# Attention scores from two float32r parts on two halves of the partitions, in place of three bfloat16 parts

## The chip, the cores and the metric

The kernel runs on one core of a Trainium2 chip. The metric is device microseconds of one launch; less is better. The page and the trace call the engines PE (TensorE's matmuls), PEld (its weight loads), DVE (VectorE), ACT (ScalarE), POOL (GpSimd) and SP (SyncE, which here only issues DMAs).

## What is computed

A transformer of two layers on `x` of 4 sequences (batches) x 1024 tokens x 128 features, all in float32. Cut to what matters:

```
x = x + attn0(layernorm(x))      # 16 heads of 8 features, causal mask, softmax, then Wo
x = x + experts(layernorm(x))    # router softmax, top 2 of 8 experts, 352 hidden
x = x + attn1(layernorm(x))      # 16 query heads, 4 key/value heads, no mask; q, k times a rotary-like factor
x = x + ffn(layernorm(x))        # 512 hidden, a sine term, relu
scores = q @ k^T;  weights = softmax(scores / sqrt(128));  out = weights @ v      # per head, 1024 x 1024
```

## The kernel before

The engines run programs of their own and meet only at semaphores. The stages follow one another: projection of layer 0 (`project(0)`), attention 0, experts, projection of layer 1, attention 1, feed-forward.

**The split.** TensorE multiplies bfloat16 faster than float32, so `project` writes each of q and k as a sum of three bfloat16 parts (SPL = 3): ACT rounds the first part (line 873), DVE subtracts it (line 1126), ACT rounds the second (line 882), DVE takes the rest (line 1130). POOL writes the parts to DRAM (`write_parts`, lines 451 and 453). SP loads them back (`load`, lines 344 and 348) so that the 8 features of a head stand in 72 partitions: the 3 x 3 products of parts, 8 rows each, are summed by one matmul with a contraction of 72 rows. That is `Q[0:CROSS, slot, j, :]` and `K[0:CROSS, slot, j, :]`, CROSS = 72, for head j of a quad.

**The work of attention.** A quad is four heads (j = 0 to 3) of one batch; there are 4 batches x 4 quads = 16 quads in each layer, g = 4b + q. Per quad there are two passes over the scores:

- `pass_a` (lines 560 to 576): for each head and each block i of 128 queries, the scores of 128 queries x all keys go to two PSUM banks, and DVE takes the maximum of each row (`row_max`, line 1152). 32 such units per quad; head j changes only after 8 units. In layer 0 only keys up to the diagonal are computed, and a matmul of the bfloat16 identity with a triangle of -1e30 (line 574) adds the mask.
- `pass_b` (lines 593 to 609): the transposed scores, 128 keys x up to 512 queries, of the heads j = 0, 1, 2, 3 in turn. Three more rows (72 to 74) hold minus the row maximum in three parts, and ones on the other side, so that the matmul subtracts it. ACT takes the exponential (line 921). In layer 0 the diagonal block gets its mask from line 607.
- `pv` (lines 611 to 624): the weights times V, in float32, four heads side by side in four groups of 32 array columns (line 620).

The row maximum gets there by `negmax_split` on DVE (lines 1155 to 1166), `negmax_turn` on PE (line 629), a copy on ACT (line 905) and one DMA from SP (`negmax_rows`, line 355).

**The order.** PE, DVE and ACT all follow one list of letters per layer (`ORDERS`, lines 147 to 151): `b` one head of pass B, `a` one unit of pass A of the next quad, `p` one `pv`, and letters for the turns. PE runs it in this order:

```
if ev[0] == "B":
    pass_b(g, q, ev[1], ev[2])
elif ev[0] == "A":
    ...
elif ev[0] == "PV":
    pv(g, q, ev[1])
```

Before the first quad, 40 units of pass A run alone (lines 643 to 652). The batches are a hardware loop on each engine (`Fori`, line 694 on PE), the last one written out.

Of the kernel before, what the change touches and what calls it, by code (L numbers as in the profile page):

```python
# [18 lines left out]
F32 = mybir.dt.float32  # L19
BF16 = mybir.dt.bfloat16  # L20
# [4 lines left out]
P = 128  # L25
# [16 lines left out]
SPL = 3  # L42
CROSS = SPL * SPL * HD
KROWS = CROSS + SPL
SLOTS = 4
PR = 8
HALF = 512
# [7 lines left out]

TWO_ONES = float(np.uint32(0x3F803F80).view(np.float32))
# [102 lines left out]
QUAD_LOADS = 2 * SPL * SPL + 1  # L159


def build(nc, h_in, Wqvk, Wo0, router_w, gate_proj, up_proj, down_proj, w_q, w_k, w_v, w_o, g_rms,
          W1, b1, phases, w_real, w_imag, W2, b2, rope, out):
    q_parts = [nc.dram_tensor(f"q_parts{l}", (SPL, P, B * S), BF16, kind="Internal").ap() for l in range(2)]
    k_parts = [nc.dram_tensor(f"k_parts{l}", (SPL, r, B * S), BF16, kind="Internal").ap()
               for l, r in enumerate((P, KV * HD))]
    x_dram = h_in.rearrange("b (t p) d -> p (b t) d", p=P)
    out_dram = out.rearrange("b (t p) d -> p (b t) d", p=P)

    with ExitStack() as ctx:  # L170
# [3 lines left out]
        def sem(name):  # L174
            return ctx.enter_context(nc.semaphore(name))
# [5 lines left out]
        Q = sb("Q", [P, SLOTS, 4, S], BF16)  # L181
        K = sb("K", [P, SLOTS, 4, S], BF16)
# [4 lines left out]
        negmax = sb("negmax", [P, SPL, 32], BF16)  # L187
        negrest = sb("negrest", [P, 32])
        negmaxT = sb("negmaxT", [SPL * 32, P], BF16)
        rden = sb("rden", [P, 4, 4])  # L190

        spare = Q[:, :, :, :].rearrange("p s j n -> p (s j n)").bitcast(F32)
# [5 lines left out]
        spare_k = K[:, :, :, :].rearrange("p s j n -> p (s j n)").bitcast(F32)  # L198
# [3 lines left out]
        identb = sb("identb", [P, P], BF16)  # L202
        causal = sb("causal", [P, P], BF16)
# [39 lines left out]
        rest = probs[:, 2:4, :]  # L243
        parts = spare[:, B * S:B * S + 2 * SPL * GW].bitcast(BF16)\
            .rearrange("p (two a c n) -> p two a c n", two=2, a=2, c=SPL)
# [20 lines left out]

        def score_a(n):
            return ps[:, 2 * n:2 * n + 2, :].rearrange("p b n -> p (b n)")

        def turn_bank(unit):  # L270
# [8 lines left out]
        consts, k_ones = sem("consts"), sem("k_ones")  # L279
# [3 lines left out]
                 "qk_sb", "v_taken", "hi_done", "rest_done", "mid_done", "split_done", "scores", "max_done",  # L283
                 "negmax_ready", "negmaxT_psum", "negmaxT_ready", "negmax_rows", "scoresT", "exp_done", "pv_done",
                 "o_copied", "o_turned", "attn_done")
        from_one = ("rstd_ready", "qk_sb", "v_taken", "rest_done", "split_done", "o_copied", "o_turned",
# [29 lines left out]
        def ones_rows(a, b):  # L316

            return K[64:96, a:b, :, :].rearrange("p s j n -> p (s j n)").bitcast(F32)
# [7 lines left out]
        def _(sp):  # L326
# [6 lines left out]
            for l in range(2):  # L333
                sl = s[l]

                def load(b, q):

                    for a in range(SPL):

                        heads = q_parts[l][a, :, bass.ts(b, S)].rearrange("(h i) n -> i h n", i=HD)  # L340
                        heads = heads[:, 4 * q:4 * q + 4, :] if l == 0 else heads[:, q:H:KV, :]
                        for r in range(SPL):
                            row = (a * SPL + r) * HD
                            sp.dma_start(Q[row:row + HD, q, :, :], heads).then_inc(loaded[l][q], 16)

                            keys = k_parts[l][r, :, bass.ts(b, S)].rearrange("(h i) n -> i h n", i=HD)
                            keys = keys[:, 4 * q:4 * q + 4, :] if l == 0 else keys[:, q:q + 1, :]
                            sp.dma_start(K[row:row + HD, q, 0:keys.shape[1], :], keys).then_inc(loaded[l][q], 16)
                    w = (HD + 1) * (4 if l == 0 else 1)
                    sp.dma_start(V[:, q, :, 0:w], v1[:, bass.ts(b, 8), w * q:w * q + w]).then_inc(loaded[l][q], 16)  # L350

                def negmax_rows(q, g):

                    sp.wait_ge(sl["negmaxT_ready"], g + 1)
                    sp.dma_start(Q[CROSS:KROWS, q, :, :].rearrange("c j (i n) -> c (j i) n", n=P),
                                 negmaxT[:, :]).then_inc(sl["negmax_rows"], 16)


                sp.wait_ge(k_ones, 2)
# [3 lines left out]
                for q in range(2):  # L363
                    load(0, q)
# [4 lines left out]
                load(0, 2)  # L369
                negmax_rows(0, 0)  # L370

                def batch(b, final):
                    for q in range(4):
                        g = 4 * b + q
                        if q == 0 or not final:
                            sp.wait_ge(sl["o_turned"], 2 * g + AT_ONE)
                            load(b if q == 0 else b + 1, (q + 3) % 4)
# [3 lines left out]
                with sp.Fori(0, B - 1) as b:  # L381
                    batch(b, False)
# [9 lines left out]
        def _(pool):  # L392
            own = Chain(pool, pool_own, own_wait=True)
            own.done(pool.memset(ident[:, :], 0.0))
            own.done(pool.memset(identb[:, :], 0.0))
            own.done(pool.memset(causal[:, :], 0.0))
# [3 lines left out]
            for m in (ident, identb):  # L400
                pool.affine_select(out=m[:, :], in_=m[:, :], compare_op=ALU.not_equal, fill=1.0, base=0,
                                   pattern=[[-1, P]], channel_multiplier=1).then_inc(consts, 1)
            pool.affine_select(out=causal[:, :], in_=causal[:, :], compare_op=ALU.is_ge, fill=MASKED, base=0,
                               pattern=[[-1, P]], channel_multiplier=1).then_inc(consts, 1)
# [4 lines left out]
            pool.wait_ge(consts, 5)  # L409
# [46 lines left out]
            own.done(pool.memset(ones_rows(0, 2), TWO_ONES))  # L456
# [50 lines left out]
        def _(pe):  # L507
# [6 lines left out]
            def project(l):  # L514
# [7 lines left out]
                read = sl["rest_done"] if l == 0 else sl["qk_sb"]  # L522
# [32 lines left out]
            def attention(l):  # L555
# [4 lines left out]
                def pass_a(quad, slot, j, i):  # L560
# [3 lines left out]
                    kj = j if l == 0 else 0  # L564
# [861 lines left out]
```

## Time and profile before

| what | value |
|---|---|
| median of 3 runs | 2203.51 us (2200.15 to 2205.18) |
| profiled execution, span from first to last instruction | 2193.3 us |
| profiled execution, its own time (end of the last instruction on the trace's own clock) | 2203.8 us |
| PE matmul busy | 2032.1 us, 93% |
| DVE busy | 1464.8 us, 67% |
| ACT busy | 1189.7 us, 54% |
| mean granted PE clock | 0.951 of full speed |
| stages, roughly | projection 0: to 82 us; attention 0: 82 to 650; experts: 650 to 1190; projection 1: 1190 to 1241; attention 1: 1241 to 2070; feed-forward: to the end |

The 10.5 us between span and own time lie around the first and last instruction. Busy times are unions of an engine's instructions. Ends of matmuls are modelled, so the distance between the starts of neighbouring matmuls tells the rate better than their duration does.

### The profile page before, as it was taken

To read this page: it belongs to the slowest core of one execution; us is meant where nothing else is said; L and a number is where in the kernel's file an instruction comes from. 1 tells how busy PE (TensorE), PEld (TensorE's weight loads), DVE (VectorE), ACT (ScalarE), POOL (GpSimd) and SP (SyncE) were. 2 spreads that over 40 slices of the span, in tenths; PEclk is the share of its full clock that TensorE was granted. 3 is DMA by queue.
4 is the path that set the end of the run, shared out by engine and by line. 5 is a ranking of instruction groups with operands and counts; after the bars stand their busy time and mean duration, and the time that the engine had idled before them with its cause. 6 is when DMAs were issued, how large, how long until landed. Compare 5 with 4: busy or idle time off the path is not lost. (4 is left out here: it accounts for less than half of the span.)

```text
span 2193.3 us, 38142 instructions
## 1 busy us (share of the span) xinstructions
PE 2032.1 (93%) x11744; PEld 893.1 (41%) x11744; DVE 1464.8 (67%) x2435; ACT 1189.7 (54%) x2374; POOL 142.6 (7%) x216
## 2 busy tenths in 40 slices
PE   4599899999999999999999789999999999999876
PEld 2244344344435666666665212222222222222355
DVE  5677577577744545455554988887886887886186
ACT  2256466466672222222322337776776777777776
POOL 3100000000000000000000100000000000000065
PEclk9689899799999999999998869999998999999998
DMA  7533324143100000000000411011111111100000
GB/s 205 129 43 38 48 27 51 28 50 41 12 2 1 0 0 0 0 0 0 0 0 1 115 15 16 16 16 17 18 26 17 16 15 16 16 2 1 1 15 24
DMA packets 75282, 56.82 MB, mean 26 GB/s; under 512 B 43120, under 2 KB 57328, under 8 KB 75120
## 3 DMA queue, kind: packets, MB, share of 16 engines
q1 hardware_dynamic: 64416, 38.62, 12.0%
q0 software_dynamic: 3072, 10.23, 1.4%
q10 hardware_dynamic: 7632, 5.88, 1.0%
q8 instruction: 93, 1.52, 0.3%
q14 instruction: 69, 0.57, 0.1%
HBM read 38.65 MB, written 12.32 MB: 23 GB/s over the span
## 5 line engine op out<-in xcount | busy, mean ns | idle before, releaser
L1152 DVE TENSOR_REDUCE rowmax<-ps 128x1 f32<-128x1024 f32 (+7 forms) x1024 | 971.3, 987 | 288.3 <-PE ps L571 140.0
L921 ACT ACTIVATE probs<-ps 128x512 f32<-128x512 f32 (+3 forms) x1792 | 860.2, 558 | 367.8 <-PE ps L604 217.1
L604 PE MATMUL ps<-Q,K 75*128 75x512 bf16 (+3 forms) x1792 | 547.5, 366 | 32.6 <-ACT probs L921 16.8
L571 PE MATMUL ps<-K,Q 72*128 72x512 bf16 (+3 forms) x1792 | 545.6, 380 | 34.7 <-DVE rowmax L1152 31.0
L620 PE MATMUL ps<-probs,V 128*9 128x512 f32 (+3 forms) x3584 | 450.2, 561 | 0.0
L604 PEld LDWEIGHTS ps<-Q,K 75*128 75x128 bf16 x1792 | 167.3, 99 | 398.7 <-ACT probs L921 281.3
L957 ACT ACTIVATE Q<-ps 128x512 f32<-128x512 f32 (+1 forms) x192 | 114.4, 596 | 324.5 <-PE ps L730 314.0
L571 PEld LDWEIGHTS ps<-K,Q 72*128 72x128 bf16 x1792 | 152.5, 100 | 326.4 <-DVE rowmax L1152 188.9
L1266 DVE TENSOR_TENSOR Q<-ps,Q 128x512 f32<-128x512 f32 (+1 forms) x192 | 130.2, 688 | 136.6 <-PE ps L733 136.4
L733 PE MATMUL ps<-Q,wu 128*128 (+3 forms) x384 | 197.2, 595 | 1.6 <-DVE Q L1266 1.6
L730 PE MATMUL ps<-Q,wg 128*128 (+3 forms) x384 | 196.9, 594 | 1.0 <-DVE attn L1177 1.0
L742 PEld LDWEIGHTS ps<-wd,Q 128*128 128x128 f32 (+1 forms) x1536 | 180.3, 191 | 28.3 <-issue 25.1
L742 PE MATMUL ps<-wd,Q 128*128 128x128 f32 (+1 forms) x1536 | 180.5, 274 | 0.0
L1278 DVE SCALAR_TENSOR_TENSOR x<-ps,ew,x 128x128 f32 (+1 forms) x256 | 72.2, 344 | 117.6 <-PE ps L742 117.6
L620 PEld LDWEIGHTS ps<-probs,V 128*9 128x9 f32 x3584 | 61.0, 89 | 149.2 <-ACT probs L921 85.6
L574 PE MATMUL ps<-causal,identb 128*128 128x128 bf16 x512 | 116.9, 231 | 0.0
L733 PEld LDWEIGHTS ps<-Q,wu 128*128 128x128 f32 (+1 forms) x384 | 68.0, 181 | 101.4 <-issue 83.1
L416 POOL TENSOR_SCALAR rtmp<-mv 128x4 f32<-128x4 f32 x16 | 3.4, 213 | 1601.8 <-DVE mv L1073 1601.8
L607 PE MATMUL ps<-identb,causal 128*128 128x128 bf16 x512 | 106.8, 225 | 0.0
L730 PEld LDWEIGHTS ps<-Q,wg 128*128 128x128 f32 (+1 forms) x384 | 65.2, 181 | 68.2 <-issue 68.2
L511 PE MATMUL ps<-ident,tokens 128*128 128x128 f32 x192 | 32.8, 298 | 42.5 <-DVE tokens L1106 30.1
L574 PEld LDWEIGHTS ps<-causal,identb 128*128 128x128 bf16 x512 | 52.4, 102 | 40.2 <-issue 8.4
(157 smaller groups left out, 1132.0 us busy)
## 6 DMA issues: line engine op xcount, KB each, us to landing
Q<-q_parts SPq DMA_DIRECT2D x288, 64.0 KB
K<-k_parts SPq DMA_DIRECT2D x144, 64.0 KB
q_parts<-Q POOLq DMA_DIRECT2D x16, 384.0 KB, 3.4
k_parts<-Q POOLq DMA_DIRECT2D x8, 384.0 KB, 7.6
V<-v SPq DMA_DIRECT2D x16, 144.0 KB
K<-k_parts SPq DMA_DIRECT2D x144, 16.0 KB
x<-in_L_attn_h_dram SPq DMA_DIRECT2D x4, 512.0 KB, 9.7
out_dram<-y SPq DMA_DIRECT2D x8, 256.0 KB, 2.3
```

The source lines that it names most:

```text
L571: last = pe.matmul(buf[:, c:e], Q[0:CROSS, slot, j, i * P:(i + 1) * P], K[0:CROSS, slot, kj, c:e], start=True, stop=not diag)
L574: last = pe.matmul(buf[:, w - P:w], identb[:, :], causal[:, :], start=False, stop=True)
L604: last = pe.matmul(ps[:, bank, c:HALF], K[0:KROWS, q, kj, t * P:(t + 1) * P], Q[0:KROWS, q, j, h * HALF + c:(h + 1) * HALF], start=True, s ...
L607: last = pe.matmul(ps[:, bank, c:c + P], causal[:, :], identb[:, :], start=False, stop=True)
L620: last = pe.matmul(ps[32 * j:32 * j + rows, PV_BANK, c:HALF], V[:, q, t, kj * rows:(kj + 1) * rows], probs[:, (4 * m + j) % PR, c:HALF], s ...
L730: pe.matmul(ps[0:w, par, :], wg[:, e, f:f + w], moving, start=True, stop=True).then_inc(moe["gate"], 1)
L733: pe.matmul(ps[0:w, 2 + par, :], wu[:, e, f:f + w], moving, start=True, stop=True).then_inc(moe["up"], 1)
L742: last = pe.matmul(ps[:, 4 + e % 2, k * D:(k + 1) * D], acts[0:w, e % 2, c, k * P:(k + 1) * P], wd[0:w, c, e, :], start=(c == 0), stop=(c ...
L921: act.activation(probs[:, (4 * m + j) % PR, c:HALF], ps[:, B_BANKS[(4 * m + j) % 3], c:HALF], ACT.Exp, scale=SCALE).then_inc(sl["exp_done" ...
L957: act.activation(gated[0:w, par, :], ps[0:w, par, :], ACT.Silu).then_inc(moe["silu"], 1)
L1152: dve.tensor_reduce(rowmax[:, par, 8 * j + i:8 * j + i + 1], score_a(i % 2)[:, 0:hd.keys(i)], AX, ALU.max).then_inc(sl["max_done"], 1)
L1266: dve.tensor_tensor(acts[0:w, e % 2, c, :], ps[0:w, 2 + par, :], gated[0:w, par, :], ALU.mult)\
```

## The change

SPL becomes 2 and the parts are float32 words. The first part is rounded by a write as float32r; the second is the float32 remainder. Q and K are float32r tiles. A head now needs 2 x 2 x 8 = 32 rows (ROWS), then one row (32) that is zero in Q and K, then two rows for minus the row maximum (KROWS = 35). Even heads stand at partitions 0 to 34, odd heads at 64 to 98 (LANE = 64), and Q and K have two heads' columns per slot in place of four. `pass_a` uses the 32 rows alone; `pass_b` all 35. The masks of layer 0 are two matmuls of 64 rows each in place of one of 128, on the half of the head. In the program, a matmul of pass A covers 32 rows x 128 columns of the array, one of pass B and of the masks 64 x 128, `pv` 128 x 32 as before, turns 128 x 128; before, all but `pv` were 128 x 128.

```diff
-SPL = 3
-CROSS = SPL * SPL * HD
+SPL = 2
+ROWS = SPL * SPL * HD
+CROSS = ROWS + 1
 KROWS = CROSS + SPL
+LANE = 64
...
-        Q = sb("Q", [P, SLOTS, 4, S], BF16)
-        K = sb("K", [P, SLOTS, 4, S], BF16)
+        Q = nc.alloc_sbuf_tensor_at("Q", [P, SLOTS, 2, S], F32R, offset=q_at)
+        K = nc.alloc_sbuf_tensor_at("K", [P, SLOTS, 2, S], F32R, offset=k_at)
...
+        def lane(j, rows):
+
+            return slice(LANE * (j % 2), LANE * (j % 2) + rows)
...
-                        last = pe.matmul(buf[:, c:e], Q[0:CROSS, slot, j, i * P:(i + 1) * P],
-                                         K[0:CROSS, slot, kj, c:e], start=True, stop=not diag)
+                        last = pe.matmul(buf[:, c:e], Q[lane(j, ROWS), slot, j // 2, i * P:(i + 1) * P],
+                                         K[lane(j, ROWS), slot, kj, c:e], start=True, stop=not diag)
                         if diag:
-                            last = pe.matmul(buf[:, w - P:w], identb[:, :], causal[:, :],
-                                             start=False, stop=True)
+                            for part in range(2):
+                                last = pe.matmul(buf[:, w - P:w], identb[lane(j, LANE), part, :],
+                                                 causal[lane(j, LANE), part, :], start=False, stop=part == 1)
...
-                    last = pe.matmul(ps[:, bank, c:HALF], K[0:KROWS, q, kj, t * P:(t + 1) * P],
-                                     Q[0:KROWS, q, j, h * HALF + c:(h + 1) * HALF], start=True, stop=not diag)
+                    last = pe.matmul(ps[:, bank, c:HALF], K[lane(j, KROWS), q, kj, t * P:(t + 1) * P],
+                                     Q[lane(j, KROWS), q, j // 2, h * HALF + c:(h + 1) * HALF],
+                                     start=True, stop=not diag)
                     if diag:
-                        last = pe.matmul(ps[:, bank, c:c + P], causal[:, :], identb[:, :],
-                                         start=False, stop=True)
+                        for part in range(2):
+                            last = pe.matmul(ps[:, bank, c:c + P], causal[lane(j, LANE), part, :],
+                                             identb[lane(j, LANE), part, :], start=False, stop=part == 1)
...
-                    for n in range(2):
-                        r = rows[n]
-                        act.wait_ge(sl["rest_done"], 2 * u + n + 1 + AT_ONE)
-                        act.activation(parts[0:r, half, n, 1, :], rest[0:r, n, :], ACT.Copy)\
-                            .then_inc(sl["mid_done"], 1)
```

Further parts, in words. `load` issues 8 DMAs for Q, 8 for K (each of 16 partition rows' worth of 4 KB instead of 32 of 2 KB) and 1 for V, 17 in place of 19; `negmax_rows` issues two DMAs, one per half. The first use of each slot also copies the zero row (2 DMAs), and 8 small DMAs at the start fill it in K from zeros in `probs`. DVE fills `probs` and K at the start over all partitions, POOL sets up the masks in 5 selects in place of 3. `negmax_split` has 2 operations in place of 4, and the row maxima are turned as a 128 x 128 float32 tile. SP's first batch is written out.

The PE program in a quad of layer 0 (one head of pass A, of pass B, and the start of a `pv`), before:

```order
L571 MATMUL ps<-K,Q 128x256 [waits max_done0]
L574 MATMUL ps<-causal,identb 128x128
L601 REGISTER_ALU
L604 MATMUL ps<-Q,K 128x384 [waits exp_done0]
L607 MATMUL ps<-identb,causal 128x128
L620 MATMUL ps<-probs,V 9x512 [waits exp_done0,o_copied0]
```

and now:

```order
L600 MATMUL ps<-K_50,Q_49 128x256 [waits max_done0]
L604 MATMUL ps<-causal,identb 128x128 x2
L631 REGISTER_ALU
L634 MATMUL ps<-Q_49,K_50 128x384 [waits exp_done0]
L639 MATMUL ps<-identb,causal 128x128 x2
L652 MATMUL ps<-probs,V 9x512 [waits exp_done0,o_copied0]
```

The order of the work is the same; each mask has become two matmuls.

The DVE program of one group of 512 tokens in the projection of layer 0, before (`probs` is the remainder, `Q` the parts):

```order
L1123 ISA
L1126 TENSOR_TENSOR probs<-ps,Q 128x512 [waits hi_done0,split_done0]
L1125 REGISTER_ALU
L1126 TENSOR_TENSOR probs<-ps,Q 128x512 [waits hi_done0]
L1130 TENSOR_TENSOR Q<-probs,Q 128x512 [waits mid_done0] x2
```

and now (`spare` is the parts):

```order
L1153 ISA
L1154 TENSOR_TENSOR spare<-ps,spare 128x512 [waits hi_done0]
L1153 REGISTER_ALU
L1154 TENSOR_TENSOR spare<-ps,spare 128x512 [waits hi_done0]
```

Two of four subtractions are gone, and the wait for ACT's second rounding with them.

## Rows read from the trace of the kernel before

**Rows 1.** The page, section 1: busy us (share of the span) xinstructions

```profile
PE 2032.1 (93%) x11744; PEld 893.1 (41%) x11744; DVE 1464.8 (67%) x2435; ACT 1189.7 (54%) x2374; POOL 142.6 (7%) x216
```

**Rows 2.** Busy by stretch (start:end, length, then each engine), attention 0, then 1

```profile
303.00:368.00 65.00, 64.32 (x533) 28.99 (x532) 48.86 (x81) 42.48 (x103) 0.00 (x0) 1.00 0.35 43
...
1531.00:1675.00 144.00, 142.34 (x799) 41.16 (x799) 118.80 (x121) 105.27 (x203) 0.00 (x0) 1.00 0.12 18
```

**Rows 3.** Timeline (start us, us), SP's DMA of the row maxima, one per quad

```profile
322.99 0.78 SPq L355 DMA_DIRECT2D Q<-negmaxT  x1
355.48 0.79 SPq L355 DMA_DIRECT2D Q<-negmaxT  x1
...
1579.42 0.78 SPq L355 DMA_DIRECT2D Q<-negmaxT  x1
1627.22 0.80 SPq L355 DMA_DIRECT2D Q<-negmaxT  x1
```

**Rows 4.** Timeline, PE in a quad of attention 1

```profile
1561.64 1.05 PE L620 MATMUL ps<-probs,V 128*9 128x512 f32 x8
1562.62 0.61 PE L571 MATMUL ps<-K,Q 72*128 72x512 bf16 x2
1563.07 0.60 PE L604 MATMUL ps<-Q,K 75*128 75x512 bf16 x2
1563.50 0.60 PE L636 MATMUL ps<-ident,oT 128*128 128x128 f32 x4
1563.94 0.38 PE L604 MATMUL ps<-Q,K 75*128 75x512 bf16 x1
1564.25 1.40 PE L620 MATMUL ps<-probs,V 128*9 128x512 f32 x8
```

**Rows 5.** Timeline, PE in the experts' stage, float32 matmuls (two records each)

```profile
900.83 0.72 PE L742 MATMUL ps<-wd,Q 128*128 128x128 f32 x5
901.38 1.02 PE L730 MATMUL ps<-Q,wg 128*128 x2
902.24 1.02 PE L733 MATMUL ps<-Q,wu 128*128 x2
```

**Rows 6.** Timeline, PE in a quad of attention 0

```profile
603.11 0.22 PE L607 MATMUL ps<-identb,causal 128*128 128x128 bf16 x1
603.17 0.22 PE L571 MATMUL ps<-K,Q 72*128 72x128 bf16 x1
603.23 0.22 PE L574 MATMUL ps<-causal,identb 128*128 128x128 bf16 x1
```

**Rows 7.** Timeline, pass A alone before attention 1: DVE, then PE

```profile
1254.89 9.42 DVE L1152 TENSOR_REDUCE rowmax<-ps 128x1 f32<-128x1024 f32 x8
```

```profile
1258.52 2.17 PE L571 MATMUL ps<-K,Q 72*128 72x512 bf16 x4 [0.19 <-DVE rowmax L1152]
```

**Rows 8.** Busy by stretch, pass A alone; the last three are clock, DMA share, GB/s

```profile
1242.00:1278.00 36.00, 31.57 (x62) 4.02 (x62) 36.00 (x31) 0.00 (x0) 0.83 (x2) 0.50 0.18 35
```

**Rows 9.** Groups by line, DVE in the projection of layer 1 (busy us, mean ns | idle)

```profile
L1130 DVE TENSOR_TENSOR Q<-probs,Q 128x512 bf16<-128x512 f32 (+1 forms) x16 | 10.3, 682 | 0.8
L1126 DVE TENSOR_TENSOR probs<-probs,Q 128x512 f32<-128x512 f32 (+1 forms) x16 | 10.2, 678 | 2.2 <-ACT Q L873 2.2
```

**Rows 10.** Timeline, ACT in the projection of layer 1

```profile
1233.36 1.15 ACT L873 ACTIVATE Q<-probs 128x512 bf16<-128x512 f32 x2 [1.26 <-DMA k_parts<-Q]
1234.81 1.22 ACT L882 ACTIVATE Q<-probs 128x512 bf16<-128x512 f32 x2 [0.15 <-DVE probs L1126]
```

**Rows 11.** Busy by stretch in the projection of layer 0 (DMA share, GB/s at the end)

```profile
50.00:55.00 5.00, 3.38 (x17) 2.12 (x16) 1.61 (x5) 1.24 (x3) 1.52 (x2) 1.00 0.81 212
```

**Rows 12.** Timeline, DVE at the start of a new batch of attention 0

```profile
262.68 0.62 DVE L1152 TENSOR_REDUCE rowmax<-ps 128x1 f32<-128x128 f32 x2 [12.41 <-issue]
```

**Rows 13.** Groups by line and form, PEld in the experts' stage

```profile
L730 PEld LDWEIGHTS ps<-Q,wg 128*128 128x128 f32 x4 | 0.7, 190 | 0.5 <-issue 0.5
```

More of the change, by code:

```diff
@@ L19 @@
 F32 = mybir.dt.float32
+F32R = mybir.dt.float32r
 BF16 = mybir.dt.bfloat16
@@ L168, in build @@
     out_dram = out.rearrange("b (t p) d -> p (b t) d", p=P)
+    q_at, k_at = (nc.bump_sbuf(SLOTS * 2 * S * 4)[0] for _ in range(2))
     with ExitStack() as ctx:
@@ L363, in _ @@
                 for q in range(2):
-                    load(0, q)
+                    load(0, q, first=True)
                 sp.wait_ge(sl["v_taken"], NG + AT_ONE)
@@ L368, in _, with batch @@
                     sp.wait_ge(sl["parts_written"][half], 32 * (NG // 2))
-                load(0, 2)
+                load(0, 2, first=True)
                 negmax_rows(0, 0)
-                def batch(b, final):
+                def batch(b, final, fresh=False):
                     for q in range(4):
@@ L376, in batch @@
                             sp.wait_ge(sl["o_turned"], 2 * g + AT_ONE)
-                            load(b if q == 0 else b + 1, (q + 3) % 4)
+                            load(b if q == 0 else b + 1, (q + 3) % 4, first=q == 0 and fresh)
                         if q < 3 or not final:
                             negmax_rows((q + 1) % 4, g + 1)
-                with sp.Fori(0, B - 1) as b:
-                    batch(b, False)
+                batch(0, False, fresh=True)
+                with sp.Fori(0, B - 2) as b:
+                    batch(b + 1, False)
                 batch(B - 1, True)
@@ L399, in _ @@
             own.done(pool.memset(power_b[:, :], -0.5))
[L400 to L404, printed above, removed]
+            own.done(pool.affine_select(out=ident[:, :], in_=ident[:, :], compare_op=ALU.not_equal, fill=1.0, base=0,
+                                        pattern=[[-1, P]], channel_multiplier=1))
+            for par in range(2):
+                rows = slice(LANE * par, LANE * par + LANE)
+                own.done(pool.affine_select(out=identb[rows, :, :], in_=identb[rows, :, :], compare_op=ALU.not_equal,
+                                            fill=1.0, base=0, pattern=[[LANE, 2], [-1, P]], channel_multiplier=1))
+                own.done(pool.affine_select(out=causal[rows, :, :], in_=causal[rows, :, :], compare_op=ALU.is_ge,
+                                            fill=MASKED, base=0, pattern=[[LANE, 2], [-1, P]], channel_multiplier=1))
             pool.affine_select(out=lower[:, :, :], in_=lower[:, :, :], compare_op=ALU.is_ge, fill=1.0, base=0,
@@ L872, in body @@
                             src = qk32[0:r, n, :]
[L873 removed]
+                        act.activation(parts[0:r, half, n, 0, :].bitcast(F32R), src, ACT.Copy)\
+                            .then_inc(sl["hi_done"], 1)
                     act.wait_ge(sl["v_out"], u + 1)
```

141 lines of the change are left out of this document (74 added, 67 removed).

## The prediction

> **What bounds the kernel now.** The page's busy line comes first: PE 93%, DVE 67%, ACT 54% [rows 1]. It mixes stages, so the second view is the busy time of stretches inside the two attentions, which hold some 1,400 of the 2,193 us: PE is busy 64.3 of 65 us and 142.3 of 144, DVE 48.9 and 118.8, ACT 42.5 and 105.3, all at the full clock of 2.4 GHz [rows 2]. PE sets the pace, and DVE comes next at 75% and 82%. The third view is the period of a quad, the distance between two DMAs of row maxima: 32.5 us in attention 0 and 47.8 us in attention 1 [rows 3].
>
> The fourth is what PE spends a quad on, read from distances between starts. A bfloat16 matmul of 512 columns takes 0.216 us (two of L604 in 0.43 us, start to start) [rows 4]; one of 128 columns 0.06 us, mask or score alike [rows 6]. A float32 matmul of 512 columns takes 0.86 us [rows 5], and a `pv` (eight records for four heads) 0.98 us from its start to the next matmul [rows 4]: the four heads run side by side, 0.86 us in all, and 0.12 us is left over. On the way in, the matmul before `pv` takes 0.31 us in place of 0.216 [rows 4]. So going between matmuls on 128 x 128 and on 128 x 32 of the array costs **about 0.10 us each way**. With this, attention 1 adds up: 128 score matmuls x 0.216 = 27.6, 16 `pv` x 0.86 = 13.8, 32 such switches = 3.2, turns (4 in 0.44 us [rows 4], twice) 0.9: 45.5 of the 47.8 us.
>
> **The change, part by part.**
>
> *Rate of a score matmul: nothing.* The trace has none in float32r. Bounds: 0.216 us for 512 columns as in bfloat16 [rows 4], or 0.86 us as in float32 [rows 5]; in between, a turn of float32 data takes 0.11 us for 128 columns [rows 4], twice bfloat16's. I take 0.216: the float32 matmul leaves two records, each with its own weight load [rows 5, 13], since both operands have to be cut in two there, and here the program has cut them beforehand. That the contraction falls from 72 to 32 rows is worth nothing: distance follows columns. A float32 weight load lasts 0.19 us [rows 13], but such loads keep up with matmuls 0.11 us apart (five in 0.55 us [rows 5]), so they hide behind 256 columns or more.
>
> *Two heads at once: a gain.* Neighbouring matmuls on different halves may run together, as the four heads of `pv` do. But order limits it. Pass A keeps its head for 8 units, so its two matmuls lie on one half. Pass B alternates, and walking the letters I count 22 free pairs of neighbouring `b` per quad in attention 1: 22 x 0.216 = 4.8 us. In attention 0 a mask must follow its score on the same half and holds up the next head; 4 pairs are left in the unmasked groups, -0.9 us, and 24 second masks that run beside the next head's score, -1.4 us.
>
> *Masks: a cost.* 64 per quad in attention 0 become 128: 64 x 0.06 = +3.8 us [rows 6].
>
> *Switches: the largest term.* Pass A now uses 32 rows of the array, pass B and the masks 64. Walking the letters around the quad, the size of the used array changes 84 times per quad in attention 0 (22 before) and 87 times in attention 1 (32 before): 62 and 55 more. The trace shows only the switch of columns. Bounds: 0, if a change of rows is free, and 0.19 us each, if the first float32 weight load cannot be brought forward [rows 13]. I take 0.10, from the nearest row [rows 4]: +6.2 and +5.5 us per quad.
>
> The Trainium skill, "TensorEngine Tiling", Key Properties, says that changing the tiling mode, and not just the tile, drains the engine, and lists 64 and 32 rows as different modes. The 0.10 us of `pv` agrees; for rows no run here shows it. By that rule the sum is the one below, and without it the first rival.
>
> *Sum of the quads.* Attention 0: 3.8 - 1.4 - 0.9 + 6.2 = +7.7; I take +7.0, since part falls where PE waits today. Attention 1: 5.5 - 4.8 = +0.7. Times 16: +112 and +11 us. DVE (32 x 1.18 = 37.7 us plus 1.5 of small work per quad of attention 1 [rows 7]) stays below 48.5.
>
> *Pass A alone.* 40 units ahead of each attention. In attention 1 DVE sets the pace, 1.18 us a unit; PE at 1.2 GHz needs 0.86 [rows 7] plus two switches: covered. In attention 0 a unit gets a mask (0.11 us at 1.2 GHz) and two switches, partly covered by DVE: +5 us.
>
> *Projections.* In layer 1 DVE loses 16 operations of 0.68 us [rows 9], and ACT a pair of 1.22 us per group [rows 10] on the loop between them; writes go from 384 to 512 KB for q. I take -12 of at most 10.9 + 8 x 1.2 = 20.5. In layer 0 the DMAs are the limit (0.81 busy, 212 GB/s [rows 11]), with a third more bytes in fewer, larger pieces: 0, within 8 either way.
>
> *With one answer.* `negmax_split` saves 0.4 us of DVE under PE. The second DMA of row maxima adds 0.8 us on SP [rows 3] behind a load of 17 DMAs in place of 19, microseconds before the next quad needs it. Should it be late, pass B would wait first. The early fills and POOL's selects precede data from DRAM. The stalls at a new batch, DVE without instructions for 12.4 us [rows 12], stay.
>
> Sum: 112 + 11 + 5 - 12 = **+116 us**. The profiled execution took 2203.8 us itself, span 2193.3, 0.3 above the median of 2203.5. So 2320 us.
>
> **Rivals.**
>
> 1. *Changing rows is free; faster.* Then attention 1 keeps -4.8 and its neighbouring `a` and `b` may overlap too, until waits for DVE (39.2 us per quad) hold it near 43.5 us: -4.2. In attention 0 the 3.8 us of masks against 2.3 of overlap, and some of A beside B: about 0. So -67 - 12 = 2125 us, up to 2200 if pairing disappoints. It decides below 0.04 us per switch. For it: only a switch of columns is shown, where the output side changes as well. Against: the same array has to be regrouped.
>
>    The Trainium skill, "TensorE: Matmul & The Clock Gate", Part 3, lets matmuls in different row groups start 4 ns apart; this supports the pairs in either case. The trace shows it only for columns.
>
> 2. *Float32r takes two passes or more; slower.* At twice the time per column attention 1 gains 13.8 us for A and some 7 for B per quad, attention 0 some 7.7 and 6: with the switches about 690 us, 2890 in all; at four passes over 3500. For it: the turns at 0.11 us. Against: one record per matmul in the new program.
>
> 3. *The clock falls; slower.* With 72 rows and matmuls on 0.86 of 1.18 us, pass A alone stayed at 1.2 GHz for its whole length [rows 7, 8]. If the sparser attention stayed there too, each quad would gain 30 us or more: over 3100. Against: quads with `pv` ran at 2.4 GHz, and at the lower clock the stream would get denser.
>
> 4. *The halves don't run together.* Then 4.8 and 2.3 us per quad come back: 2430 us.
>
> **Numbers.** My forecast 0.50, rival 1 0.28, rival 2 0.12, rival 3 0.05, rival 4 0.05. Both signs have weight: the likeliest case alone spans 2250 to 2400. The range leaves out rivals 2 and 3: from 2115 (rival 1 in full) to 2430 (rival 4, or switches at 0.16 us). About 0.2% is what a measurement of this kernel can tell from no change. Of rival 1, 0.26 is faster and 0.02 within 0.2%; of the forecast 0.02 each for faster and same: faster 0.28, same 0.04, slower 0.68.
>
> **What would show it.** Right: a quad near 39.5 us in attention 0 and 48.5 in attention 1; neighbouring `b` 0.01 us apart and then a gap; 0.3 us from an L634 matmul of 512 columns to an L600 one. Wrong: `a` and `b` on different halves starting together (rival 1); 0.43 us or more between two L600 matmuls of one unit (rival 2); clock 0.5 in the quads (rival 3); neighbouring `b` always 0.216 apart (rival 4).

## The result and the profile after

| | before | after |
|---|---|---|
| median | 2202.79 us (4 runs, 2200.15 to 2205.18) | 3527.82 us (4 runs, 3522.27 to 3532.10) |
| ratio to before | 1 | 1.601, 95% interval 1.596 to 1.606 |
| span of the profiled execution | 2193.3 us | 3527.0 us |
| mean granted PE clock | 0.951 | 0.613 |

The change makes the kernel 60% slower. The page of after, its busy line and its clock row (one digit for each fortieth of the span, tenths of full speed):

```profile
PE 3397.6 (96%) x12768; PEld 1446.6 (41%) x12768; DVE 1480.0 (42%) x2340; ACT 1218.6 (35%) x2342; POOL 143.7 (4%) x219
...
PEclk8555555555555589999985555555555555555589
```

PE is now 96% busy, and DVE and ACT do about the same work as in [rows 1] in a span 1.6 times as long. The clock row shows why: fives through both attentions, nines in the experts' stage between them and at the very end. Stretches of attention 0 and 1, and then all of attention 1 (start:end, length, PE, PEld, DVE, ACT, POOL busy, clock, DMA share, GB/s):

```profile
303.00:368.00 65.00, 65.00 (x305) 28.75 (x299) 21.84 (x35) 19.48 (x45) 0.00 (x0) 0.50 0.15 20
...
2459.00:2557.00 98.00, 97.66 (x267) 31.35 (x265) 40.57 (x38) 36.66 (x67) 0.00 (x0) 0.50 0.07 9
...
1889.00:3406.00 1517.00, 1497.86 (x4184) 480.95 (x4180) 603.89 (x591) 584.46 (x1070) 2.43 (x4) 0.51 0.05 7
```

Against [rows 2] PE does 305 matmuls in the same 65 us where it did 533, at 0.50 in place of 1.00, and the clock stays down for 1,500 us though PE has work the whole time. The period of a quad, from SP's DMAs of the row maxima (now two at a time):

```profile
549.28 1.31 SPq L372 DMA_DIRECT2D Q<-negmaxT  x2
620.88 1.29 SPq L372 DMA_DIRECT2D Q<-negmaxT  x2
...
2458.90 1.36 SPq L372 DMA_DIRECT2D Q<-negmaxT  x2
2556.96 1.29 SPq L372 DMA_DIRECT2D Q<-negmaxT  x2
```

71.6 and 98.1 us, where [rows 3] had 32.5 and 47.8 and the forecast 39.5 and 48.5. The whole difference lies here: from its first `pv` to its last, attention 1 takes 1517 us in place of 779 (+738), and attention 0 by the same measure 1128 in place of 543 (+585): 1323 of the 1334 us between the spans. Inside a quad of attention 1, PE (start, length, line, shape, how many):

```profile
2601.47 0.79 PE L634 MATMUL ps<-Q,K 35*128 35x512 f32 x1
2602.19 1.22 PE L600 MATMUL ps<-K,Q 32*128 32x512 f32 x2
2603.33 0.79 PE L634 MATMUL ps<-Q,K 35*128 35x512 f32 x2
2604.05 1.90 PE L652 MATMUL ps<-probs,V 128*9 128x512 f32 x8
```

At half clock 512 columns take 0.43 us, twice the 0.216 of [rows 4]. The two L634 of the third line, an even and an odd head, need 0.72 us from the start of the first to `pv`: one matmul of 0.43 and 0.29 more, which is taken up below with e1. So the two halves do run together, and float32r does go in one pass. The two L600 take 1.14 us to the next line, more than two times 0.43 and one switch.

### The profile page after: what moved, and what is told of

Same layout as the page of the kernel before. It is cut to its first block and busy times, and to the rows that moved or that the text cites. A ratio compares the mean times of both kernels' runs of the same rounds, so it can differ in the third digit from the quotient of the medians.

```text
span 3527.0 us, 39737 instructions
## 1 busy us (share of the span) xinstructions
PE 3397.6 (96%) x12768; PEld 1446.6 (41%) x12768; DVE 1480.0 (42%) x2340; ACT 1218.6 (35%) x2342; POOL 143.7 (4%) x219
## 5 line engine op out<-in xcount | busy, mean ns | idle before, releaser
L600 PE MATMUL ps<-K,Q 32*128 32x512 f32 (+3 forms) x1792 | 1036.2, 663 | 19.6 <-DVE rowmax L1176 17.7
L634 PE MATMUL ps<-Q,K 35*128 35x512 f32 (+3 forms) x1792 | 867.6, 715 | 24.5 <-ACT probs L948 14.5
L652 PE MATMUL ps<-probs,V 128*9 128x512 f32 (+3 forms) x3584 | 754.8, 938 | 0.0
L600 PEld LDWEIGHTS ps<-K,Q 32*128 32x128 f32 x1792 | 445.6, 297 | 591.0 <-issue 371.9
L634 PEld LDWEIGHTS ps<-Q,K 35*128 35x128 f32 x1792 | 360.3, 289 | 663.6 <-ACT probs L948 333.8
L764 PE MATMUL ps<-spare,wu 128*128 (+3 forms) x384 | 197.9, 597 | 1.6 <-DVE spare L1287 1.6
L761 PE MATMUL ps<-spare,wg 128*128 (+3 forms) x384 | 197.8, 597 | 1.0 <-DVE attn L1198 1.0
L604 PE MATMUL ps<-causal,identb 64*128 64x128 bf16 x1024 | 195.4, 291 | 0.0
L773 PEld LDWEIGHTS ps<-wd,spare 128*128 128x128 f32 (+1 forms) x1536 | 180.3, 191 | 28.3 <-issue 25.1
L773 PE MATMUL ps<-wd,spare 128*128 128x128 f32 (+1 forms) x1536 | 180.5, 274 | 0.0
L604 PEld LDWEIGHTS ps<-causal,identb 64*128 64x128 bf16 x1024 | 63.5, 103 | 191.0 <-issue 182.6
L652 PEld LDWEIGHTS ps<-probs,V 128*9 128x9 f32 x3584 | 60.9, 96 | 186.6 <-issue 109.6
```

The source lines that it names most:

```text
L600: last = pe.matmul(buf[:, c:e], Q[lane(j, ROWS), slot, j // 2, i * P:(i + 1) * P], K[lane(j, ROWS), slot, kj, c:e], start=True, stop=not diag)
L604: last = pe.matmul(buf[:, w - P:w], identb[lane(j, LANE), part, :], causal[lane(j, LANE), part, :], start=False, stop=part == 1)
L634: last = pe.matmul(ps[:, bank, c:HALF], K[lane(j, KROWS), q, kj, t * P:(t + 1) * P], Q[lane(j, KROWS), q, j // 2, h * HALF + c:(h + 1) * H ...
L652: last = pe.matmul(ps[32 * j:32 * j + rows, PV_BANK, c:HALF], V[:, q, t, kj * rows:(kj + 1) * rows], probs[:, (4 * m + j) % PR, c:HALF], s ...
L761: pe.matmul(ps[0:w, par, :], wg[:, e, f:f + w], moving, start=True, stop=True).then_inc(moe["gate"], 1)
L764: pe.matmul(ps[0:w, 2 + par, :], wu[:, e, f:f + w], moving, start=True, stop=True).then_inc(moe["up"], 1)
```

## The experiments

Two theories of the clock: **rows** (the stream of matmuls that drive only 32 or 35 of the array's 128 rows is granted the lower clock) and **stream** (the switches between array shapes break up the work of PE; a switch is two neighbouring matmuls on different sizes of the array). A third takes the clock for a bystander: **cost**, switches and weight loads being dearer than the forecast's. The table gives, for all kernels, the rows that a matmul of pass A, of pass B and of the masks contracts, the usual period of a quad, and the mean granted clock from the first `pv` to the last of each attention. All periods are distances between the first `pv` of neighbouring quads. Before, after and e10 are medians of four executions; each of e1 to e9 was executed once, and the differences that the readings rest on are far above the spread of those four (at most 0.8%).

| kernel | rows A / B / masks | us | att. 0: quad, clock | att. 1: quad, clock |
|---|---|---|---|---|
| before | 72 / 75 / 128, bf16 | 2202.79 | 32.5, 0.96 | 47.8, 0.98 |
| after | 32 / 35 / 64 | 3527.82 | 71.6 to 74, 0.52 | 98.1, 0.51 |
| e1_33rows | 33 / 35 / 64 | 3020.0 | 47 to 65, 0.57 | 79.1, 0.52 |
| e2_64rows | 64 / 64 / 64 | 2450.5 | 39 to 55, 0.81 | 49.0, 0.98 |
| e3_bf16_a64 | 64 / 75 / 128, bf16 | 2425.1 | 37.2, 0.89 | 52.4, 0.92 |
| e4_bf16_a32 | 32 / 75 / 128, bf16 | 2847.8 | 37 to 65, 0.75 | 65 to 95, 0.64 |
| e5_full | 128 / 128 / 64 | 2862.6 | 58 to 77, 0.71 | 51.2, 0.99 |
| e6_one_half | 64 / 64 / 64, one half only | 2720.3 | 41.0 to 74.6, 0.86 | 51.5 to 92, 0.77 |
| e7_a32_b64 | 32 / 64 / 64 | 3449.7 | 63 to 74, 0.55 | 70 to 100, 0.57 |
| e8_full_masks | 128 / 128 / 128 | 2424.26 | 40.3, 0.99 | 51.2, 0.99 |
| e9_masks64 | 72 / 75 / 64, bf16 | 2681.84 | 61 to 81, 0.65 | 47.8, 0.97 |
| e10_bf16_pairs | att. 0 as before; att. 1 64 / 64, bf16 | 2137.94 | 32.5, 0.98 | 45.7, 0.98 |

### Rows alone: e1 and e2

e1 lets pass A contract row 32 too, which is zero in Q and K. The sums are the same, but a matmul of pass A now takes 64 x 128 of the array as pass B does, and the 32/64 switches are gone:

```diff
-  Q[lane(j, ROWS), slot, j // 2, i * P:(i + 1) * P], K[lane(j, ROWS), slot, kj, c:e]
+  Q[lane(j, CROSS), slot, j // 2, i * P:(i + 1) * P], K[lane(j, CROSS), slot, kj, c:e]
```

> The changed kernel with pass A on 33 rows (the zero row included) in place of 32, so that pass A uses 64 x 128 of the array as pass B does; the same sums. Of 84 and 87 changes of the used array per quad 27 and 37 stay. Theory 'gaps' (the clock stays at 1.2 GHz because changes of the used array break the stream): the gaps go, the clock returns to 1.0 in most of the attention, and the time falls to 2200 to 2450 us. Theory 'rows' (it stays down because few of the 128 rows carry data): clock stays at 0.5; only the gaps go, 0.127 us each, 57 and 50 per quad, 16 quads: 3528 - 217 = about 3310 us, or more below if matmuls of pass A and B then overlap.

3020.0 us, with the clock at 0.57 and 0.52, so the rows theory had the clock nearly right and the time 290 us too high.

e2 has the same matmuls in the same order on the same tiles; rows 33 to 63 of each half are driven as well, with zeros in Q (K has ones there) that two more DMAs per load put there:

```diff
-  Q[lane(j, CROSS), ...], K[lane(j, CROSS), ...]       # pass A
-  K[lane(j, KROWS), ...], Q[lane(j, KROWS), ...]       # pass B
+  Q[lane(j, LANE), ...], K[lane(j, LANE), ...]
+  K[lane(j, LANE), ...], Q[lane(j, LANE), ...]
```

> As e1_33rows, but pass A and pass B contract 64 rows of their half: rows 33 (35 once the row maxima are in) to 63 of Q are zeros, written by two more DMAs per load, against ones in K. Same used array, same switches as e1; only the number of rows driven differs (64 in place of 33 and 35). Theory 'gaps': equal to e1 within 1%. Theory 'rows': the clock rises against e1 if e1 stayed at 0.5, and the time falls by several hundred us; if zeros don't count as activity, equal to e1.

The clock rows of the two pages, e1 and then e2:

```profile
PEclk9556555667555699999995555555555555555688
```

```profile
PEclk9558687788789899999999975999999999999998
```

And a stretch of 144 us in attention 1 of each, e1 and then e2:

```profile
2000.00:2144.00 144.00, 143.31 (x482) 59.01 (x482) 73.24 (x70) 64.71 (x120) 0.00 (x0) 0.50 0.09 12
```

```profile
1850.00:1994.00 144.00, 136.79 (x737) 59.05 (x735) 108.40 (x107) 97.12 (x187) 0.00 (x0) 0.96 0.12 27
```

The two programs differ on PE only in rows that add nothing to any sum, and e2 is 570 us faster although its extra DMAs let attention 0 begin at 171 us in place of 118. A quad of attention 1 goes from 79.1 to 49.0 us, the clock from 0.52 to 0.98. This shows the rows as a cause: PE's instructions are the same, and rows whose products are all zero are enough to bring the clock back. That e2's 49.0 us lie near the forecast's 48.5 is luck: e2 has 37 switches in this quad and not the forecast's 87, and its weight loads cost time that the forecast put at nothing.

e1 against after removes the 32-row tiles at one and the same clock in attention 1: 98.1 to 79.1, 19 us a quad. Two neighbouring places of e1 at 1.2 GHz, and then a place of e4 (bfloat16, 32 rows), beside the 1.14 us of after:

```profile
2045.74 1.05 PE L600 MATMUL ps<-K,Q 33*128 33x512 f32 x2
2046.72 1.90 PE L652 MATMUL ps<-probs,V 128*9 128x512 f32 x8
2048.55 1.22 PE L600 MATMUL ps<-K,Q 33*128 33x512 f32 x2
2049.69 1.90 PE L652 MATMUL ps<-probs,V 128*9 128x512 f32 x8
```

```profile
2070.31 1.03 PE L571 MATMUL ps<-K,Q 32*128 32x512 bf16 x2
2071.27 1.03 PE L604 MATMUL ps<-Q,K 75*128 75x512 bf16 x2
```

In e4 two 32-row matmuls and a switch take 0.96 us, in after 1.14. In e1 the same pair takes 0.98 us where the matmul before it was on its own shape, and 1.14 where it follows a `pv`. So it is not the 32 rows: what matters is whether a switch lies just before. Measured over attention 1, the second of two float32r matmuls behind a switch, where the two don't run side by side, starts 0.59 us after the first at 1.2 GHz, in all 464 places of after and all 82 of e6 (64 rows); at 2.4 GHz 0.34 us, in all 185 places of e6 and all 230 of e8 (128 rows). Further on in a run it is 0.43 at 1.2 GHz (449 of 457 places in e6) and mostly 0.23 at 2.4 GHz. Bfloat16 shows nothing of this (0.23 us behind a switch in e3, 0.40 at 1.2 GHz in e4). The records of the weight loads fit: in after a float32r load lasts 0.28 to 0.33 us and that of the second matmul starts 0.16 us behind the first matmul, where in e4 a load lasts 0.10. So a float32r weight load comes late behind a switch, by 0.165 us at 1.2 GHz; it does so behind a pair too (0.59 us). After has such a late load in 69 places of a quad of attention 1, e1 in 19: 50 x 0.165 = 8.3 us. The switches fall from 87 to 37, and at 0.127 us each (0.554 less 0.427) that is 6.4. Together 14.7 of the 19 us. Most of the rest must be pairs that after doesn't have: in this quad of e1 a matmul of pass A and one of pass B stand within 0.11 us of each other 16 times, in after never.

The Trainium skill, "TensorE: Matmul & The Clock Gate", Part 2, step 1, says that a weight load is pulled ahead of running matmuls when the row groups do not conflict or when it goes to the background buffer, and names no difference by type. On bfloat16 the trace agrees (0.216 us apart on the same rows, [rows 4]), and on float32r inside a run of one shape it does for the most part; behind a switch a float32r load is late.

### Fewer rows in bfloat16, and wide rows in pass B alone: e3, e4, e7

e3 and e4 leave the kernel before in bfloat16 and only let pass A contract the first 64 or 32 of the 72 rows:

```diff
-  Q[0:CROSS, slot, j, i * P:(i + 1) * P], K[0:CROSS, slot, kj, c:e]
+  Q[0:64, slot, j, i * P:(i + 1) * P], K[0:64, slot, kj, c:e]      # e4: 0:32
```

> The kernel before, with pass A on 64 of its 72 rows (the products of the third part with the third part are left out of the row maximum). Pass A then uses 64 x 128 of the array, all else of the scores 128 x 128: switches around every run of pass A (and in attention 0 between each score and its mask), no halves, no float32r. The switch costs 0.105 us at full clock as in the changed kernel: 62 and about 39 more per quad, +6.5 and +4 us, 16 quads: +170 us if the clock stays up. Theory 'gaps': the clock falls as well and the time goes beyond 2800 us. Theory 'rows': rows fall only from 72 to 64 in pass A, the clock stays at 0.9 or more, 2350 to 2400 us.

> As e3_bf16_a64 with pass A on 32 rows (the row maximum is taken from the first four of nine products). The number of switches is that of e3. Theory 'gaps': the same time and clock as e3 within 1%. Theory 'rows': the clock is lower than in e3 for part of the attention, above all in attention 1 where pass A takes 29% of PE's time, and the time is longer.

e3 came out 25 us above the range of the rows theory: 2425.1 us.

e3 is the price of the switches without a large fall of the clock: 37.2 less 32.5 and 52.4 less 47.8, +4.7 and +4.6 us a quad. Neighbours at 2.4 GHz show it singly: 0.31 us from a matmul of pass A to one of pass B and back, 0.216 to 0.226 within a pass. So 0.09 to 0.10 us for a change of rows, as for a change of columns, and in bfloat16 the forecast's price of a switch is right. In float32r the late load behind a switch comes on top.

e4 has the same switches as e3 and fewer rows. Stretches of 200 us in attention 1, e3 and then e4:

```profile
2000.00:2200.00 200.00, 198.51 (x1013) 42.00 (x1011) 150.83 (x152) 138.76 (x259) 0.00 (x0) 1.00 0.08 13
```

```profile
2000.00:2200.00 200.00, 194.72 (x620) 29.25 (x620) 94.78 (x93) 87.44 (x159) 0.00 (x0) 0.58 0.05 9
```

The clock falls with bfloat16 too, by the rows alone, so float32r isn't needed for it; and e8 below, in float32r, has 0.99, so float32r isn't enough for it. In e4 the clock moves between the levels, where after stayed at the lower one.

e7 is e2 with pass A back on 32 rows, pass B on 64:

```diff
-  Q[lane(j, LANE), slot, j // 2, i * P:(i + 1) * P], K[lane(j, LANE), slot, kj, c:e]
+  Q[lane(j, ROWS), slot, j // 2, i * P:(i + 1) * P], K[lane(j, ROWS), slot, kj, c:e]
```

> From e2_64rows with pass A on 32 rows as in the changed kernel, pass B on 64 (zeros added): the switches of the changed kernel, but 64 rows in pass B. Theory 'rows': between the changed kernel (3528) and e2 (2450), with a clock between 0.52 and 0.9 in the quads; about 2900 to 3300 us. Theory 'gaps' would give 3528 again.

Raising the rows of pass B alone helps little (3449.7 us against 3527.82, and above the expected 2900 to 3300): with 32/64 switches and narrow matmuls in half of the stream, the clock stays at 0.55 and 0.57. A wide pass A with a narrow pass B was not run.

e7 shows what the quads of after would cost at the full clock. At the lower level its half quads of attention 1 last 45.1 and 52.9 us, exactly those of after (98.1 together). Once each, they were granted the higher one (second half, first half):

```profile
2051.10:2082.20 31.10, 30.50 (x140) 11.22 (x139) 21.83 (x24) 18.69 (x36) 0.00 (x0) 0.99 0.01 4
3138.90:3164.50 25.60, 25.60 (x131) 9.00 (x132) 17.66 (x16) 17.54 (x32) 0.00 (x0) 1.00 0.00 1
```

From first `pv` to first `pv` they took 25.6 and 31.2 us. So a quad of after at 2.4 GHz is about 56.8 us, an estimate from these two halves: 41.3 of the 98.1 us are the clock, and the cost theory accounts for the 8.3 us between 56.8 and the forecast's 48.5.

### Rows do not suffice: e5, e8, e9

e5 goes from e2 to all 128 partitions for the scores. Each sum then holds two heads, so it isn't the reference's. The masks remain on 64 rows:

```diff
-  Q[lane(j, LANE), slot, j // 2, ...], K[lane(j, LANE), slot, kj, ...]
+  Q[0:P, slot, j // 2, ...], K[0:P, slot, kj, ...]
```

> From e2_64rows: pass A and pass B contract all 128 partitions, both halves at once, on 128 x 128 of the array, still float32r. The scores are then sums over two heads (not the reference's); the same number of matmuls and columns, but no pairs, no change of the used array in attention 1. Theory 'rows': clock 1.0 in attention 1, also in the stage of pass A alone (1.2 GHz before with 72 rows). Rate: if float32r streams as bfloat16 and its weight loads hide on the full array, a quad of attention 1 takes 47.8 us as before; if the load is exposed as it is in e2 (0.34 in place of 0.216 us), up to 60. Two passes would give 75 or more.

Here the expectation missed twice. Pass A alone ahead of attention 1 stays at 0.50 with all 128 rows driven, in e5 and in e8, where the rows theory said 1.0; rows don't change that stage. Attention 1 behaves (51.2 us, 0.99), and float32r takes about 0.23 us per 512 columns, one pass, and 0.34 behind a switch; on the full array it costs 3.4 us a quad more than the bfloat16 of before. But attention 0, with the masks, has a clock of 0.71 with all rows driven, lower than e2's 0.81 with half of them. What e5 has and e2 has not is a switch of rows between each score and its mask. e8 puts the masks on 128 rows as well, in the same number of matmuls:

```diff
-  identb[lane(j, LANE), part, :], causal[lane(j, LANE), part, :]
+  identb[0:P, part, :], causal[0:P, part, :]
```

> The run e5_full with its masks contracting all 128 partitions as well (still two matmuls for each diagonal block, their sums doubled; the score sums hold two heads, so the output is not the reference's). No change of rows is left between a score and its mask. Theory (a stream broken by changes of the array's rows holds the clock down as few rows do): attention 0 loses 128 changes of 0.10 us a quad and stays at a granted clock of 0.95 or more, quads of 34 to 40 us in place of 57 to 77, 2400 to 2480 us in all in place of 2862.6. Rival (the float32r scores themselves, or the masks being two, hold it down): the clock of attention 0 stays near 0.7, quads of 45 us and more, 2650 us or more. Attention 1 has no masks: 51 us a quad by both.

200 us of attention 0, e5 and then e8:

```profile
400.00:600.00 200.00, 197.94 (x1015) 91.31 (x1013) 80.61 (x118) 76.08 (x159) 0.00 (x0) 0.80 0.15 27
```

```profile
400.00:600.00 200.00, 196.47 (x1596) 116.98 (x1595) 121.38 (x184) 109.06 (x249) 0.00 (x0) 0.98 0.24 43
```

The quads fall to 40.3 us at 0.99, where they had 58 to 77 at 0.71, and attention 1 doesn't change. e9 is the counter-test on the kernel before, in bfloat16 and with 72 and 75 rows; only its masks become two matmuls on 64 rows each:

```diff
-  pe.matmul(buf[:, w - P:w], identb[:, :], causal[:, :], start=False, stop=True)
+  for part in range(2):
+      pe.matmul(buf[:, w - P:w], identh[0:64, part, :], causalh[0:64, part, :], start=False, stop=part == 1)
```

> The kernel before (bfloat16, scores on 72 and 75 rows) with each mask of attention 0 as two matmuls of 64 rows on the same half, in place of one of 128; nothing else. Per quad 64 masks, so 128 changes of rows more at 0.10 us and 64 matmuls of 0.06 us: 32.5 + 12.8 + 3.8 = 49 us a quad at an undisturbed clock, and with 16 quads 2470 us in all. Theory (changes break the stream and the clock falls with it): the clock of attention 0 falls clearly below 0.9, quads of 52 to 75 us, 2550 to 2850 us. Rival (only the rows driven count; 72 rows are the same as before): clock 0.93 or more, about 49 us a quad. Attention 1 is unchanged, 47.8 us.

```profile
400.00:600.00 200.00, 198.37 (x1048) 60.87 (x1052) 83.89 (x128) 75.60 (x162) 0.00 (x0) 0.68 0.19 23
```

At an undisturbed clock the 128 switches and 64 small matmuls would have given about 49 us; the quads take 61 to 81, at a clock of 0.65, and the total rises by 488 us against the 2193.75 of before measured beside it. The scores keep their rows; the masks go from 128 rows to 64, but that doesn't explain 0.65, since e2 and e6 have the same masks and scores on 64 rows too, without a switch between them, and were granted 0.81 and 0.86. So switches bring the clock down as well. Both theories hold, and the change does both: it takes rows away and adds switches.

### The halves together: e6

e6 is e2 with the odd heads on the even half as well (their sums are those of the even heads), so no two matmuls can run side by side:

```diff
-  return slice(LANE * (j % 2), LANE * (j % 2) + rows)
+  return slice(0, rows)
```

> From e2_64rows: all heads are read from the even half (odd heads compute the even heads' scores, half of the causal mask is missing), so nothing can run in pairs; rows, used array and counts as in e2. Pairs are worth 22 x 0.216 = 4.8 us per quad of attention 1 and about 2 in attention 0 by my sum: 2450 + 110 = 2560 us. If a matmul also waits for the weight load of its own half, each of the lost pairs costs 0.34 and the time goes to 2650 us or more.

At clock 1.0 a quad of attention 1 takes 51.5 us against e2's 49.0: all pairs of e2 together, those of pass A with pass B among them, are worth 2.5 us, where the forecast counted 4.8 for pass B alone. The pairs were there as counted (21 in a quad of after, 0.004 us apart), but the load behind a pair is late. The total of 2720.3 us is above the expected 2560 to 2650, because the clock falls: 0.77 in attention 1 against e2's 0.98, with the same rows and switches. What differs is that only one half of the array works at a time, and neither theory foresaw a lower clock from that; in attention 0 it is the other way round (0.86 against 0.81), so whether this is the cause is open. And e6 visits both levels with one program. Two stretches of attention 1:

```profile
2100.00:2200.00 100.00, 95.37 (x284) 44.03 (x282) 43.47 (x42) 38.78 (x70) 0.00 (x0) 0.53 0.07 15
...
2300.00:2400.00 100.00, 99.37 (x516) 48.08 (x516) 76.09 (x75) 68.44 (x130) 0.00 (x0) 1.00 0.12 27
```

The quad that lies at 0.50 takes 91.9 us (others at 0.53 take 88.5) and the one at 1.00 takes 51.5, a factor of 1.8. That is the price of the clock for this kind of quad, measured without any change of program.

The trace also shows when the clock falls here. Both falls inside attention 1 of e6 (at 1857 and 2106 us) come right behind a pause of PE at a change of batch; the first:

```profile
1852.54 0.66 PE L673 MATMUL ps<-ident,oT 128*128 128x128 f32 x4
1856.61 1.11 PE L640 MATMUL ps<-Q,K 64*128 64x512 f32 x3 [3.42 <-issue]
```

These pauses (3 to 4 us between two starts) are in every kernel; what differs is how long the lower clock lasts behind them in attention 1: 7 and 14 us in before, 7 to 10 in e2 and e8, 44 and 51 in e3, 89 and 181 in e6. After enters attention 1 at the lower clock, from pass A alone, and practically never leaves it. In attention 0 of e5 and e9, and in e4, the clock also falls without such a pause, near the same places of one quad after another.

### A version that beats both: e10

What was left to gain was the pairs, if rows, switches and weight loads could be kept in order. e10 is the kernel before with attention 1 alone changed: bfloat16, six of the nine products of parts (48 rows; the three smallest are left out), three rows for the maximum, zeros up to 64, one head of a pair on each half. All scores of attention 1 then have one shape, only `pv` and the turns have others, and attention 0 keeps its full masks.

```diff
+                        if l == 1:
+                            last = pe.matmul(buf[:, c:e], Q[lane(j, LANE), slot, j // 2, i * P:(i + 1) * P],
+                                             K[lane(j, LANE), slot, 0, c:e], start=True, stop=True)
+                            continue
```

> A candidate: the kernel before, but in attention 1 alone the scores are bfloat16 on two halves of 64 rows: 6 of the 9 products of parts (the three smallest are left out), 48 rows, three for the maximum and rows of zeros up to 64, in pass A and pass B. 28 DMAs a load in place of 19. Attention 0 is unchanged. Theory (pairs of halves are worth what e6_one_half less e2_64rows gave, 2.5 us a quad; bfloat16 weight loads stay hidden; the clock stays up with 64 rows driven, as in e2_64rows): 44 to 46.5 us a quad in attention 1 in place of 47.8, 2150 to 2185 us in all. Rival (64 rows in place of 75 let the clock fall for a part of attention 1, as it was 0.92 in e3_bf16_a64): 48 to 52 us a quad, 2200 to 2280 us.

2137.94 us (2134.44 to 2150.97, 4 runs) against 2193.75 of before measured beside it: ratio 0.976, interval 0.971 to 0.980. Its clock row, DMAs of row maxima, and PE in a quad of attention 1:

```profile
PEclk9689999899999999999999859999999999999998
```

```profile
1356.75 1.61 SPq L393 DMA_DIRECT2D Q<-negmaxT  x2
1402.45 1.56 SPq L393 DMA_DIRECT2D Q<-negmaxT  x2
```

```profile
1603.43 1.05 PE L672 MATMUL ps<-probs,V 128*9 128x512 f32 x8
1604.41 0.40 PE L652 MATMUL ps<-Q,K 64*128 64x512 bf16 x2
1604.64 0.59 PE L615 MATMUL ps<-K,Q 64*128 64x512 bf16 x2
1605.07 0.38 PE L652 MATMUL ps<-Q,K 64*128 64x512 bf16 x1
```

Two L652 together take 0.23 us where [rows 4] had 0.43 for two L604, and two L615 of one head 0.43 as before: no weight load shows. The period is 45.7 us in place of 47.8, and attention 1 takes 744 us in place of 779: 35 us. The time came out below the expected 2150 to 2185, by a part that the pairs don't explain. In the profiled executions attention 1 also begins 19 us earlier. 13 of these lie in the quads of attention 0, where the program is the same: two that took 41.5 and 41.6 us in before take 33.6 and 36.4. Before shows the lower clock in such a place, its 41.5 us quad at a change of batch being in the first line:

```profile
260.00:300.00 40.00, 36.59 (x273) 16.34 (x274) 25.91 (x44) 21.63 (x52) 0.00 (x0) 0.87 0.13 21
```

```profile
260.00:300.00 40.00, 39.62 (x328) 17.80 (x326) 29.70 (x50) 27.63 (x66) 0.00 (x0) 1.00 0.29 36
```

(before, then e10). The lower clock lasts 17 and 24 us behind the first two changes of batch of attention 0 in before, and 7 and 14 in e10. Whether that is chance of the two executions or comes with e10 is open.

## Why the prediction was wrong

The direction was right, the size was not: +1325 us against +116, outside the range of 2115 to 2430. By its steps:

- **The step that failed is the silent assumption that the quads stay at the full clock, and with it rival 3, held at 0.05.** It named what happened ("each quad would gain 30 us or more: over 3100"), with pass A alone at 0.50 as its witness [rows 8] (a weak one: e8's pass A alone stays at 0.50 with 128 rows too). I set against it that the quads with `pv` ran at 2.4 GHz and would get denser. But those were quads of 72 and 75 rows with 22 and 32 switches; the change alters both at once, and neither argument carried over. Being denser in time didn't help: PE was 99% busy through attention 1 at 0.51. The Trainium skill, "TensorE: Matmul & The Clock Gate", Part 1, says that the lower level is the default and activity releases the higher one. The traces agree on the two levels; being busy for 99% of the time did not bring the higher one here.
- *Size of it.* In attention 1, from 98.1 us: 41.3 are the clock, by e7's halves at the full one, and the 56.8 left are 8.3 more than the forecast's 48.5. By another path, 19.0 go with the 32-row tiles (e1) and 30.1 with the rows driven at the same tiles (e1 to e2), all of it clock.
- *Rate of a float32r matmul: right*, about 0.23 us for 512 columns, one pass. *Its weight load: wrong.* I priced it at nothing from loads behind 0.11 us matmuls [rows 5]. Directly behind a switch or a pair it is late, by 0.165 us at 1.2 GHz and 0.10 to 0.12 at 2.4, on 32, 64 and 128 rows alike. In the experts' stage all matmuls have one shape, so [rows 5] could not show it. This is about what the forecast's work lacks, 8 us a quad.
- *Switches: right in bfloat16*, 0.10 us each at 2.4 GHz for rows as for columns (e3). In float32r the late load doubles that, to 0.20 to 0.22 us, just past the 0.19 us that I had as the upper bound and set aside. And that switches cost more than their own time, through the clock, is what e5, e8 and e9 show; the forecast had no such term. Rival 1 falls with it.
- *Pairs: right in kind*, and 22 a quad as counted, but worth about half, since the load behind a pair is late (2.5 us for all pairs of e2, by e6). Rival 4 falls. With 2.5 in place of 4.8 the forecast would have been 37 us higher, not more.
- *Rival 2 falls*: one pass. (Its own terms, 16 x 34.5 us and the forecast's 116, add up to 668 us, not 690.)
- *Projection of layer 1.* From the last operation of the experts (start 1190.01 and 1783.22) to the first row maximum (1240.78 and 1830.70) it takes 47.5 us in place of 50.8: -3.3, not -12. DVE's saving is there, but it then waits for ACT:

```profile
1822.35 1.28 DVE L1154 TENSOR_TENSOR spare<-probs,spare 128x512 f32<-128x512 f32 x2 [1.69 <-ACT spare L904]
...
1829.49 1.28 DVE L1154 TENSOR_TENSOR spare<-probs,spare 128x512 f32<-128x512 f32 x2 [4.47 <-ACT spare L904]
1830.70 2.34 DVE L1176 TENSOR_REDUCE rowmax<-ps 128x1 f32<-128x1024 f32 x2
1833.22 2.36 DVE L1176 TENSOR_REDUCE rowmax<-ps 128x1 f32<-128x1024 f32 x2 [0.18 <-PE ps L600]
```

- *Pass A alone: nearly.* Attention 0 begins 6 us later (126 for 120), as forecast. In attention 1 I called it covered; a unit takes 1.26 us (two in 2.52, last lines above, against 1.18 in [rows 7]), PE being the slower now through the weight loads: about +4 us.

What stays open: the split of attention 0, where rows, tiles and masks change together, isn't measured one by one; why e6's clock is below e2's; and why, behind pauses of the same length, the clock comes back after 89 us in one place of e6 and after 181 in another.

## What to carry to other kernels

Before narrowing what TensorE contracts, or cutting its work into several array shapes, read the granted clock as a resource that the present shapes earn: a quad of the same program (e6) cost 51.5 us at the one level and 91.9 at the other, more than any saving in the work itself. Rows of zeros are cheap in time and gave the clock back (3020.0 to 2450.5 us, e1 to e2), and a small mask on another shape took it away (e9, +488 us). If two row halves are wanted, keep every neighbouring matmul on that one shape and the type one whose weight loads are hidden, as in e10.

## What the runs showed of the hardware that was not expected

- TensorE 99% busy was granted 1.2 GHz for 1,500 us. With zeros in some 30 more rows per matmul and one shape for all scores the clock was 0.98.
- With all 128 rows driven by the scores, small masks on 64 rows between them brought the clock to 0.71 (e5); the same masks on 128 rows gave 0.99 (e8).
- Behind pauses of 3.5 to 4 us between two matmul starts in attention 1 the lower clock lasted 7 us in e8 and up to 181 us in e6, with PE busy for 99% of those 181 us.
- Behind a switch a float32r weight load was late by 0.165 us at 1.2 GHz and 0.10 to 0.12 at 2.4 GHz, on 32, 64 and 128 rows (e7, e6, e8); in bfloat16 two matmuls on the same rows stood 0.216 to 0.226 us apart at 2.4 GHz whether on 72, 64 or 32 rows.
- A switch of rows costs 0.10 us at 2.4 GHz (e3) and 0.11 in bfloat16 (e4) or 0.127 in float32r (after) at 1.2 GHz, so it doesn't double with half the clock.
